# Experts of an expert-choice FFN: tokens fetched by indirect transfers instead of one-hot gather products

## The chip, the cores and the metric

One core of a Trainium2 chip runs the whole program, a four-layer model whose stages follow one another. The metric is the device time of one execution in microseconds.

## The reference, cut to what matters

Layer 2 holds an FFN in which every expert chooses its tokens. With n = 8 batches, t = 256 x 2 = 512 tokens, d = 256, hidden f = 1024, 8 experts:

```python
scores = jnp.einsum('ntd,ed->nte', x, gate_w)
probs = jax.nn.softmax(scores, axis=-1)
g, m = jax.lax.top_k(probs.transpose(0, 2, 1), k)     # k = 2 * 512 / 8 = 128 tokens of each expert and batch
xin = x[batch_idx, m]                                  # [8, 8, 128, 256]
h = jax.nn.gelu(jnp.einsum('nekd,edf->nekf', xin, w1), approximate=False)
h = jnp.einsum('nekf,efd->nekd', h, w2)
out = jnp.zeros((n, t, d), dtype=x.dtype).at[batch_idx, m].add(g[..., None] * h)
```

`x` here is the layer-normed activation `xn`. The layer's output is x + s * silu(out), with s the output of a causal attention over the same `xn`.

## The kernel before, in words

The engines are programmed by hand: each stage is a block with one instruction stream per engine, joined by semaphores, and a barrier of all engines ends it. The stages that matter run in this order:

- **The causal attention** (`stage_causal_attend`, L2566). TensorE makes scores for groups of four heads, VectorE takes row maxima, ScalarE exponentiates. A step handles one group g of one batch b; there are 32. SyncE loads the q, k and v stacks of batch b + 1 as the groups of batch b end (L2638 to L2643). Beside this, VectorE finds the 128 best tokens of each of the 64 pairs of batch and expert (`ExpertChoice.dve`, L2251) with sixteen rounds of three operations, and sets `found` after the last. At the beginning SyncE loads the probabilities, w1 and w2 of expert 0 and the first two batches of xn (`load_ahead`, L2230); after the last attention load it stores the places in DRAM and reads the first two rows of them spread over all partitions (`spread_places`, L2237).
- **The gather products** (`experts_gather`, L2863). Per batch, VectorE splits xn in two fp32r parts (high and low), and makes the one-hot matrix `picks` by comparing the places with the number of each token (L2911). TensorE multiplies: for two halves of d and two halves of the experts, four token tiles times two parts, 128x512 each (L2930): 32 products a batch, 256 in all. ScalarE copies the results to `slots` (L2899), which holds the chosen tokens of all experts and batches, d in the partitions. TensorE also turns the probabilities and places (L2918, L2919).
- **The experts' FFN** (`experts_ffn`, L2936). A unit is one half k of the batches (4 x 128 tokens) of one expert e; 16 units. The operands are pairs of fp32r parts and each product has three passes (`three_passes`, L461; its products stand on L464). In step f of a unit TensorE makes the second product of the unit before (12 products of 128x256, banks 4 to 7) and the first product of this one (6 products of 128x512, banks 0 to 3). ScalarE takes the gelu (L2982). VectorE splits the hidden tile (L448 and L455), splits a slice of w2 (k = 0) or of the next expert's w1 (k = 1), at step 3 splits the next unit's x from `slots` (`split_x`, L3000), and at step 1 copies the output of the last-but-one unit to `slots`, times the probabilities (`outputs`, L3008, L3014). GpSimd has nothing to do. SyncE loads the next expert's weights and, once, the weights of the stage after the next into `choice.late` (`distance.load`, L2165).
- **The scatter** (`experts_scatter`, L3082) adds the outputs to their tokens by one-hot products, with silu on ScalarE and the gating on GpSimd; it reads `place_t`, a slot's tokens in its partition.

## Time and profile before

| what | us |
|---|---|
| median of 3 runs (lowest, highest) | 3902.56 (3898.4, 3906.61) |
| the profiled execution, its own time | 3910.28 |
| its span, first to last instruction | 3908.6 |
| TensorE busy in the span | 3289.4 (84%) |
| VectorE busy | 3101.5 (79%) |
| ScalarE busy | 2306.6 (59%) |
| GpSimd busy | 1647.5 (42%) |

The profile shows one execution. Times on its timeline count from the span's start; a comparison with the runs goes by the execution's own time. PE is TensorE's products, PEld its weight loads, DVE VectorE, ACT ScalarE, POOL GpSimd, SP SyncE; a q behind a name (SPq) is an engine's queue of instructions. A product's duration is longer than its distance to the next one, since products overlap.

### The profile page before, as it was taken

The page shows a single profiled execution, that of the slowest core. Times are in us where ns is not written, and L with a number is a line of the kernel's source. Part 1 is how long each engine was busy: PE and PEld are TensorE (multiplying, and loading weights), DVE is VectorE, ACT ScalarE, POOL GpSimd, SP SyncE. Part 2 cuts the span into 40 slices and gives each one's busy share as a digit, 9 for nine tenths or more (in the row PEclk, how much of TensorE's full clock was granted, in tenths as well). Part 3 has the DMA queues.
Part 4 walks back from the last instruction along what each step waited for, and adds up shares of the span by engine and source line. Part 5 has one row for each costly group of instructions (what it writes and reads, how often), then busy time and mean ns, then how long its engine had stood idle before and what let it go on. Part 6 is the DMA issues. An engine that isn't in the chain of part 4 may idle for free. (4 is left out here: it accounts for less than half of the span.)

```text
span 3908.6 us, 57210 instructions
## 1 busy us (share of the span) xinstructions
PE 3289.4 (84%) x16866; PEld 1768.0 (45%) x16866; DVE 3101.5 (79%) x4970; ACT 2306.6 (59%) x2770; POOL 1647.5 (42%) x785
## 2 busy tenths in 40 slices
PE   6758888888979997869799999799996977777776
PEld 3322333333337876645333343599985751111111
DVE  6869999999987777847589885487767768888887
ACT  4767666666663336724266666222222758999998
POOL 0009998989963110022100000000015338998996
PEclk9879999999999998968699999899998987888888
DMA  4543333333303357838532322221103553344442
GB/s 124 199 192 125 116 131 140 141 141 141 117 30 109 124 153 183 196 106 272 161 79 70 75 73 54 81 64 54 43 28 113 170 174 94 114 124 123 122 117 90
DMA packets 294398, 465.54 MB, mean 119 GB/s; under 512 B 40711, under 2 KB 237960, under 8 KB 273790
## 3 DMA queue, kind: packets, MB, share of 16 engines
q1 hardware_dynamic: 249838, 412.98, 33.0%
q10 hardware_dynamic: 44432, 51.10, 4.9%
q8 instruction: 50, 0.82, 0.1%
q14 instruction: 78, 0.64, 0.1%
HBM read 322.44 MB, written 141.33 MB: 119 GB/s over the span
## 5 line engine op out<-in xcount | busy, mean ns | idle before, releaser
L1225 PE MATMUL mamba_psum<-mamba_hc,scan_ident 128*128 128x512 f32 x1024 | 547.3, 642 | 91.7 <-DVE mamba_hc L1133 74.3
L3643 POOL TENSOR_TENSOR distance_dist<-distance_dist,distance_least_all 128x2048 f32<-128x2048 f32 x124 | 559.1, 4540 | 74.6 <-DMA distance_least_all<-distance_least_rows 74.6
L3126 POOL TENSOR_TENSOR scatter_out<-scatter_out,scatter_s 128x512 f32<-128x512 f32 x16 | 28.0, 1756 | 1032.4 <-ACT scatter_out L3143 1018.0
L1156 DVE TENSOR_TENSOR_SCAN mamba_psum<-mamba_psum,mamba_drive 128x512 f32<-128x512 f32 x352 | 414.8, 1216 | 23.2 <-issue 10.8
L2704 DVE TENSOR_REDUCE causal_row_max<-causal_psum 128x1 f32<-128x512 f32 x512 | 333.2, 683 | 81.5 <-PE causal_psum L2774 72.1
L1225 PEld LDWEIGHTS mamba_psum<-mamba_hc,scan_ident 128*128 128x128 f32 x1024 | 174.8, 195 | 419.3 <-DVE mamba_hc L1133 258.1
L2663 ACT ACTIVATE causal_probs<-causal_psum 128x1024 f32<-128x1024 f32 x256 | 250.9, 1021 | 125.3 <-PE causal_psum L2797 125.2
L3819 PE MATMUL distance_psum<-distance_shared_k_stacks,distance_shared_q_stacks 102*128 102x512 bf16 x512 | 207.8, 502 | 116.6 <-DVE distance_least L3737 56.5
L3737 DVE TENSOR_REDUCE distance_least<-distance_psum 128x2 f32<-128x1024 f32 x256 | 294.1, 1213 | 7.6 <-PE distance_psum L3819 7.3
L3773 DVE TENSOR_SCALAR distance_dist<-distance_psum 128x1024 f32<-128x1024 f32 x192 | 227.0, 1219 | 81.0 <-PE distance_psum L3834 81.0
L1076 POOL TENSOR_TENSOR mamba_drive<-late_channels,scan_b_all 128x1024 f32<-128x1024 f32 x64 | 150.0, 2357 | 287.9 <-POOLq L32 287.9
L1120 ACT ACTIVATE mamba_psum<-mamba_dt,scan_a_neg 128x512 f32<-128x512 f32 x256 | 167.4, 683 | 141.0 <-DVE mamba_hc L1133 140.5
L1120 ACT ACTIVATE mamba_psum<-late_channels,scan_a_neg 128x512 f32<-128x512 f32 x256 | 167.2, 683 | 137.3 <-DVE mamba_hc L1133 129.2
L2982 ACT ACTIVATE ffn_hidden<-experts_psum 128x512 f32<-128x512 f32 x128 | 76.7, 599 | 281.8 <-PE experts_psum L464 281.8
L3714 ACT ACTIVATE distance_dist<-distance_dist 128x2048 f32<-128x2048 f32 x128 | 233.8, 1898 | 0.3
L2773 PE MATMUL causal_psum<-causal_shared_k_stacks,causal_shared_q_stacks 100*128 100x512 bf16 x512 | 194.6, 405 | 29.3 <-DVE causal_row_max L2704 14.7
L1156 DVE TENSOR_TENSOR_SCAN mamba_h<-mamba_psum,mamba_drive 128x512 f32<-128x512 f32 x160 | 193.9, 1212 | 4.6 <-ACT mamba_psum L1120 4.6
L3706 ACT ACTIVATE distance_dist<-distance_dist 128x2048 f32<-128x2048 f32 x96 | 179.3, 1899 | 6.0 <-DVE distance_dist L3773 5.7
L2796 PE MATMUL causal_psum<-causal_shared_q_stacks,causal_shared_k_stacks 103*128 103x512 bf16 x512 | 170.6, 385 | 3.1 <-ACT causal_probs L2663 1.6
L3819 PEld LDWEIGHTS distance_psum<-distance_shared_k_stacks,distance_shared_q_stacks 102*128 102x128 bf16 x512 | 34.3, 105 | 300.3 <-DVE distance_least L3737 198.7
L3855 PE MATMUL distance_psum<-distance_dist,distance_shared_v 128*32 128x512 f32 x1024 | 158.6, 698 | 12.1 <-ACT distance_dist L3714 10.5
L3834 PE MATMUL distance_psum<-distance_shared_q_stacks,distance_shared_k_stacks 102*128 102x512 bf16 x512 | 142.1, 398 | 14.7 <-DVE distance_dist L3773 11.9
(477 smaller groups left out, 8776.0 us busy)
## 6 DMA issues: line engine op xcount, KB each, us to landing
distance_least_all<-distance_least_rows SPq DMA_DIRECT2D x32, 1024.0 KB, 4.6
scan_b_all<-bc SPq DMA_DIRECT2D x16, 1024.0 KB, 4.7
scan_c_all<-bc SPq DMA_DIRECT2D x16, 1024.0 KB, 6.7
mamba_b_all<-bc SPq DMA_DIRECT2D x16, 1024.0 KB, 5.0
mamba_c_all<-bc SPq DMA_DIRECT2D x16, 1024.0 KB, 6.9
choice_w<-L_ffn_w SPq DMA_DIRECT2D x16, 1024.0 KB, 5.6
z<-mamba_in_z SPq DMA_DIRECT2D x8, 1024.0 KB, 3.9
xc<-mamba_in_xc SPq DMA_DIRECT2D x8, 1024.0 KB, 3.9
```

Of the source, the lines that this page charges most:

```text
L1120: act.activation(ps[:, DECAY_BANK + n % RING], dt[slot][:, m], ACT.Exp, scale=a_neg[:, m, s:s + 1]).then_inc(decay_ready, 1)
L1156: dve.tensor_tensor_scan(out, bank, drive[:, n % DRIVES], 0.0, ALU.mult, ALU.add).then_inc(h_ready, 1)
L1225: pe.matmul(ps[:, Y_BANK + m % 2], ident[:, :], hc[:, n % PRODUCTS], start=False, stop=(s == DS - 1)).then_inc(y_summed, 1)
L2663: act.activation(probs[:, g % 2, kt, 2 * pair:2 * pair + 2], ps[:, 2 + n % 2 * 2:4 + n % 2 * 2], ACT.Exp, scale=SCALE).then_inc(p_ready, 1)
L2704: dve.reduce_max(row_max[:, g % 2, u:u + 1], ps[:, u % 2], AX.X).then_inc(a_max, 1)
L2773: pe.matmul(ps[:, u % 2], qs[0:KA, g, h, i * P:(i + 1) * P], ks[0:KA, g, h, :], start=True, stop=False)
L3643: pool.tensor_tensor(dist[:, g % 2, kt], dist[:, g % 2, kt], least_all[:, g % 2], ALU.subtract).then_inc(shifted, 1)
L3706: act.activation(dist[:, g % 2, kt], dist[:, g % 2, kt], ACT.Sqrt).then_inc(sqrt_ready, 1)
L3714: act.activation(dist[:, g % 2, kt], dist[:, g % 2, kt], ACT.Exp, scale=-1.0).then_inc(p_ready, 1)
L3737: dve.tensor_reduce(least[:, g % 2, h * TT + 2 * j:h * TT + 2 * j + 2], ps[:, pair(UNITS + u)], op=ALU.min, axis=AX.X).then_inc(a_min, 1)
L3773: dve.tensor_scalar(dist[:, g % 2, kt, j * 2 * T:(j + 1) * 2 * T], ps[:, pair(u)].rearrange("p h t -> p (h t)"), D2_MIN, None, ALU.max).th ...
L3819: last = pe.matmul(ps[:, pair(UNITS + u)][:, i], qs[0:KD, g, h, (2 * j + i) * P:(2 * j + i + 1) * P], ks[0:KD, g, h, :], start=True, stop= ...
```

## The change

The stage of gather products is gone. The attention's SyncE stores the places before the loads for the last batch, and reads them back transposed (`turn_places`), so that partition j has the j-th token of every pair of batch and expert. GpSimd adds each batch's first row number, converts to integers and fetches for expert 0 the 128 rows of xn of every batch by indirect transfers (`gather`, 128 partitions x 256 f32 each): 4 for each half k, into `raw`, which has one buffer per half. In the FFN GpSimd fetches the rest, 4 transfers after each unit's rows have been turned, 56 in all. A unit's rows are turned on TensorE at steps 3 and 4 of the unit before, four 128x128 blocks a step, into banks 4 to 7, the two that do not collect the present second product. ScalarE rounds each bank into x high, VectorE subtracts it from the bank into x low. Four of the six late weight matrices are loaded where all were, the other two and `wo` after the last turn, since `raw` lies in their place. The removed functions stand in full in the section above; of the diff the new code follows.

```diff
...
+    def load_rest(self, sp):
+        self.load_rows(sp, self.NAMES[self.BELOW_RAW:])
         load_head_columns(sp, self.wo_cols, self.w["wo"], self.loaded)
...
+        self.raw = self.late[:, 2 * TT * D:].rearrange("p (k n d) -> p k n d", k=2, n=NB // 2)
+        self.place_t = c.sb("place_t", [P, NB * NE2])
+        self.first_row = c.sb("first_row", [P, NB * NE2])
+        self.rows = c.sb("rows", [P, NB * NE2], mybir.dt.uint32)
...
-    def spread_places(self, sp):
+
+    def turn_places(self, sp, nc):
         sp.wait_ge(self.found, 1)
-        sp.dma_start(self.place_dram.rearrange("b (e j) -> (b e) j", e=NE2), self.place_f[:, :]).then_inc(self.place_stored, DMA)
+        sp.dma_start(self.place_dram, self.place_f[:, :]).then_inc(self.place_stored, DMA)
         sp.wait_ge(self.place_stored, DMA)
-        for r in range(2):
-            self.load_places(sp, r, r)
+        with nc.allow_non_contiguous_dma(reason="a slot's tokens to its partition, once"):
+            sp.dma_start(self.place_t[:, :], self.place_dram.rearrange("r j -> j r")).then_inc(self.place_loaded, DMA)
 
     def pool(self, pool):
         make_identity(pool, self.ident, self.ident_made)
-        pool.iota(self.token[:, :], [[P, TT]], base=0, channel_multiplier=1,
-                  allow_small_or_imprecise_dtypes=True).then_inc(self.made, 1)
         pool.iota(self.tokens[:, :], [[1, T]], base=0, channel_multiplier=0,
                   allow_small_or_imprecise_dtypes=True).then_inc(self.made, 1)
+        pool.iota(self.first_row[:, :], [[T, NB], [0, NE2]], base=0, channel_multiplier=0,
+                  allow_small_or_imprecise_dtypes=True).then_inc(self.made, 1)
+        pool.wait_ge(self.made, 2)
+        pool.wait_ge(self.place_loaded, DMA)
+        pool.tensor_tensor(self.first_row[:, :], self.place_t[:, :], self.first_row[:, :], ALU.add).then_inc(self.rows_ready, 1)
+        pool.wait_ge(self.rows_ready, 1)
+        pool.tensor_copy(self.rows[:, :], self.first_row[:, :]).then_inc(self.rows_ready, 1)
+        pool.wait_ge(self.rows_ready, 2)
+        for k in range(2):
+            self.gather(pool, 0, k)
+
+    def gather(self, pool, e, k):
+
+        rows = self.xn_in.rearrange("b t d -> (b t) d")
+        for n in range(NB // 2):
+            column = (k * (NB // 2) + n) * NE2 + e
+            pool.indirect_dma_start(
+                out=self.raw[:, k, n, :], out_offset=None, in_=rows,
+                in_offset=bass.IndirectOffsetOnAxis(ap=self.rows[:, column:column + 1], axis=0)).then_inc(self.gathered[k], DMA)
 
...
+                choice.load_ahead(sp)
+                with sp.Fori(0, NB - 2) as b:
+                    load_next(b)
+                choice.turn_places(sp, nc)
+                load_next(NB - 2)
...
-        experts_gather(nc, choice, ps, prob_t, place_t, slots)
...
+        TURN_STEPS = (3, 4)
+
+        def following(e, k):
+            return (e, 1) if k == 0 else (e + 1, 0)
+
+        def turned_bank(k, m):
+            return ps[:, 4 + 2 * (1 - k) + m]
...
-                distance.load(sp, nc)
+                distance.load_first(sp, nc)
                 with sp.Fori(1, NE2 - 1) as e:
                     load_next(e)
+                sp.wait_ge(x_turned, UNITS * DT)
+                distance.load_rest(sp)
+
+            @block.gpsimd
+            def _(pool):
+                for e in range(1, NE2):
+                    for k in range(2):
+                        pool.wait_ge(x_turned, ((e - 1) * 2 + k + 1) * DT)
+                        choice.gather(pool, e, k)
 
             @block.scalar
             def _(act):
+                def round_x(e, k, m):
+
+                    act.wait_ge(x_turned, (e * 2 + k) * DT + m + 1)
+                    act.copy(x_parts.high[:, k, :, m * P:(m + 1) * P],
+                             turned_bank(k, m).rearrange("p (n j) -> p n j", n=HB)).then_inc(x_parts.rounded, 1)
+
                 def body(e, final):
                     for n in range(2 * FT2):
+                        k, f = divmod(n, FT2)
                         tile = e * 2 * FT2 + n
                         act.wait_ge(h_done, tile + 1)
                         wait_past(act, h_parts.ready, tile + 1 - RAW)
                         act.activation(hidden[:, n % RAW], ps[:, n % 4], ACT.Gelu).then_inc(h_ready, 1)
-
+                        if f in TURN_STEPS and not (final and k == 1):
+                            round_x(*following(e, k), TURN_STEPS.index(f))
+
+                act.wait_ge(prob_turned, 1)
+                act.copy(prob_t[:, :], ps[:, 0, 0:NB * NE2]).then_inc(prob_copied, 1)
+                for m in range(DT):
+                    round_x(0, 0, m)
...
+                def rest_of_x(e, k, m):
+
+                    dve.wait_ge(x_parts.rounded, (e * 2 + k) * DT + m + 1)
+                    rows = slice(m * P, (m + 1) * P)
+                    dve.tensor_tensor(x_parts.low[:, k, :, rows], turned_bank(k, m).rearrange("p (n j) -> p n j", n=HB),
+                                      x_parts.high[:, k, :, rows], ALU.subtract).then_inc(x_parts.ready, 1)
...
-                        if f == 3 and not (final and k == 1):
-                            split_x(e + k, 1 - k)
+                        if f - 1 in TURN_STEPS and not (final and k == 1):
+                            rest_of_x(*following(e, k), TURN_STEPS.index(f - 1))
...
+                split_w1(0, 0)
+                for m in range(DT):
+                    rest_of_x(0, 0, m)
+                for f in range(1, FT2):
                     split_w1(0, f)
-                split_x(0, 0)
+                dve.wait_ge(prob_copied, 1)
...
+                def turn_x(e, k, m):
+
+                    if m == 0:
+                        pe.wait_ge(choice.gathered[k], (e + 1) * HB * DMA)
+                        wait_past(pe, o_copied, (e * 2 + k - 2) * HB)
+                    for n in range(HB):
+                        last = pe.transpose(turned_bank(k, m)[:, n * P:(n + 1) * P], choice.raw[:, k, n, m * P:(m + 1) * P],
+                                            choice.ident[:, :])
+                    last.then_inc(x_turned, 1)
...
+                        if f == 0:
+                            pe.wait_ge(x_parts.ready, (e * 2 + k) * DT + DT)
                         if not (isinstance(e, int) and e == 0 and k == 0):
                             second_product(e - 1 + k, 1 - k, f)
+                        if f in TURN_STEPS and not (final and k == 1):
+                            turn_x(*following(e, k), TURN_STEPS.index(f))
                         first_product(e, k, f)
...
+                pe.wait_ge(choice.ident_made, 2)
+                pe.transpose(ps[:, 0, 0:NB * NE2], choice.best[:, :], choice.ident[0:NB * NE2, 0:NB * NE2]).then_inc(prob_turned, 1)
+                for m in range(DT):
+                    turn_x(0, 0, m)
+                pe.wait_ge(prob_copied, 1)
...
```

SyncE at the end of the attention, before: the place store and the two spread reads behind the last load.

```order
L2634 REGISTER_ALU
L357 ISA
L357 DMA causal_shared_v<-v 128x4x128
L2638 REGISTER_ALU
L2638 COMPARE_AND_BRANCH
L2239 DMA experts_place_rows<-choice_place_f 64x128
L2228 DMA choice_late<-experts_place_rows 128x1024 x2
```

And in the change, the same place:

```order
L357 DMA causal_shared_v<-v 128x4x128
L2663 REGISTER_ALU
L2663 COMPARE_AND_BRANCH
L2240 DMA experts_place_rows<-choice_place_f 64x128
L2243 DMA choice_place_t<-experts_place_rows 128x64x1
L339 DMA causal_shared_q_stacks<-q_parts 48x2048
L339 DMA causal_shared_q_stacks<-q_parts 32x2048
L339 DMA causal_shared_q_stacks<-q_parts 16x2048
```

The store and the transposed read now stand ahead of the loads for the last batch (written out once behind the loop).

TensorE at step 3 of the first FFN unit, in the change:

```order
L464 MATMUL experts_psum<-ffn_x_high,ffn_w_high 128x512
L464 MATMUL experts_psum<-ffn_x_low,ffn_w_high 128x512
L464 MATMUL experts_psum<-ffn_x_high,ffn_w_low 128x512
L3029 MATMUL experts_psum<-choice_ident,choice_late 128x128 x4
L464 MATMUL experts_psum<-ffn_x_high,ffn_w_high 128x512
L464 MATMUL experts_psum<-ffn_x_low,ffn_w_high 128x512
```

Before, the products followed one another without the four turns (`choice_late` is the buffer that holds `raw`). GpSimd's stream, empty in the FFN before, now has there:

```order
L2932 UNCONDITIONAL_BRANCH
L2265 DMA choice_late<-xn,choice_rows 128x256 x56
L2915 UNCONDITIONAL_BRANCH
```

## Rows read from the trace of the kernel before

**Rows 1.** Stretches: us, busy PE, PEld, DVE, ACT, POOL, then granted clock, DMA, GB/s

```profile
2447.00:2526.20 79.20, 64.97 (x258) 51.55 (x258) 35.74 (x48) 19.14 (x34) 0.00 (x0) 0.90 0.23 80
2546.80:2896.40 349.60, 349.60 (x2255) 318.76 (x2254) 258.70 (x568) 72.50 (x121) 0.00 (x0) 1.00 0.15 45
...
2690.00:2712.50 22.50, 22.50 (x146) 20.44 (x145) 17.06 (x38) 4.79 (x8) 0.00 (x0) 1.00 0.14 47
```

**Rows 2.** Timeline, borders of the gather stage: start, us, engine, line, output<-inputs

```profile
2447.05 0.34 PE L2918 MATMUL experts_psum<-choice_ident,choice_best 64*128 64x64 f32 x1 [5.59 <-PEq L32]
...
2447.20 0.69 DVE L448 CAST gather_xn_high<-choice_late 128x1024 fp32r<-128x1024 f32 x1 [12.83 <-PEq L2920]
...
2526.25 0.29 DVE L448 CAST ffn_w_high<-choice_w 128x256 fp32r<-128x256 f32 x1 [10.91 <-PEq L32]
...
2526.92 0.29 DVE L448 CAST ffn_w_high<-choice_w 128x256 fp32r<-128x256 f32 x1
```

**Rows 3.** Timeline, the head of the FFN

```profile
2532.40 1.23 DVE L455 TENSOR_TENSOR ffn_x_low<-experts_slots,ffn_x_high 128x1024 fp32r<-128x1024 f32 x1
2533.68 0.79 PE L464 MATMUL experts_psum<-ffn_x_high,ffn_w_high 128*128 128x512 f32 x1 [9.54 <-DVE ffn_x_low L455]
2534.27 0.63 PE L464 MATMUL experts_psum<-ffn_x_low,ffn_w_high 128*128 128x512 f32 x1
...
2537.27 0.43 DVE L448 CAST ffn_h_high<-ffn_hidden 128x512 fp32r<-128x512 f32 x1 [3.65 <-ACT ffn_hidden L2982]
...
2541.18 0.42 DVE L448 CAST ffn_h_high<-ffn_hidden 128x512 fp32r<-128x512 f32 x1
...
2542.90 0.42 DVE L448 CAST ffn_h_high<-ffn_hidden 128x512 fp32r<-128x512 f32 x1
...
2546.80 0.28 PE L464 MATMUL experts_psum<-ffn_w_high,ffn_h_high 128*128 128x256 f32 x1
```

**Rows 4.** Turns on L2522 (causal_in): one group, all 64, and the stretch

```profile
1872.25 1.07 PE L2522 MATMUL causal_in_psum<-means_ident,causal_in_xn 128*128 128x128 f32 x8
...
L2522 PE MATMUL causal_in_psum<-means_ident,causal_in_xn x64: 272/273/477, 1731.9 to 1873.1; 128*128 128x128 f32 x64
...
1870.00:1876.00 6.00, 4.46 (x34) 3.63 (x33) 2.38 (x8) 3.67 (x6) 3.47 (x3) 1.00 1.09 203
```

**Rows 5.** Timeline, steps 1 to 3 of one FFN unit

```profile
2710.64 0.60 ACT L2982 ACTIVATE ffn_hidden<-experts_psum 128x512 f32<-128x512 f32 x1 [2.22 <-PE experts_psum L464]
...
2711.82 0.69 DVE L455 TENSOR_TENSOR ffn_h_low<-ffn_hidden,ffn_h_high 128x512 fp32r<-128x512 f32 x1
...
2713.16 1.66 DVE L3014 TENSOR_SCALAR experts_slots<-experts_psum,experts_prob_t 128x256 f32 x4
...
2713.46 0.60 ACT L2982 ACTIVATE ffn_hidden<-experts_psum 128x512 f32<-128x512 f32 x1 [2.22 <-PE experts_psum L464]
...
2714.61 0.40 PE L464 MATMUL experts_psum<-ffn_x_high,ffn_w_high 128*128 128x512 f32 x1
```

**Rows 6.** GpSimd in the scatter stage (ns min/median/max), and a stretch of the scan

```profile
L3126 POOL TENSOR_TENSOR scatter_out<-scatter_out,scatter_s x16: 1263/1441/4877, 2911.6 to 2992.4; 128x512 f32<-128x512 f32 x16
...
500.00:900.00 400.00, 351.24 (x777) 130.20 (x776) 382.34 (x431) 264.25 (x339) 368.24 (x194) 0.97 0.33 126
```

**Rows 7.** Timeline, SyncE's issues late in the attention, TensorE's first scores of batch 7

```profile
2329.39 1.26 SPq L339 DMA_DIRECT2D causal_shared_q_stacks<-q_parts  x3
...
2346.19 0.38 PE L2773 MATMUL causal_psum<-causal_shared_k_stacks,causal_shared_q_stacks 100*128 100x512 bf16 x1
...
2390.01 0.51 SPq L2239 DMA_DIRECT2D experts_place_rows<-choice_place_f  x1
2392.46 1.10 SPq L2228 DMA_DIRECT2D choice_late<-experts_place_rows  x2
```

**Rows 8.** DMA packets, from 1688 to 1689 and from 1690 to 1692 us

```profile
DMA packets 2101, 0.09 MB, mean 88 GB/s; under 512 B 2038, under 2 KB 2100, under 8 KB 2100
...
DMA packets 872, 0.05 MB, mean 27 GB/s; under 512 B 872, under 2 KB 872, under 8 KB 872
```

108 lines of the change are left out of this document (14 added, 94 removed).

## The prediction

> **What bounds the kernel now.** I read the busy time by stretch first, since a share over the whole span says nothing of one stage. The change touches two stages that follow one another on one core. The first is the stage of gather products: it takes 79.2 us from its first instruction to the first of the experts' FFN [rows 1]. In it TensorE is busy 64.97 us, VectorE 35.74 and ScalarE 19.14, so TensorE is its bound, with starts and stops. The second is the FFN. From its second unit on TensorE is busy 349.6 of 349.6 us at full granted clock, VectorE 258.7, ScalarE 72.5 and GpSimd not at all [rows 1]: whatever the change adds to TensorE there is paid in full, and what it adds to ScalarE and GpSimd is hidden until one of them makes TensorE wait.
>
> Then the timeline at the borders. TensorE and VectorE start the gather stage at 2447.05 and 2447.20, and the FFN's first VectorE instruction stands at 2526.25 [rows 2]. In the FFN's head VectorE works alone: eight splits of w1, 0.67 us each from 2526.25 to 2526.92 [rows 2], then the split of x, which ends at 2533.63, then TensorE starts at 2533.68 [rows 3]. Its first eight products last until the second unit starts at 2546.80 [rows 3]. A unit is half the batches of one expert, 16 in all; in the steady state one step (a second product and a first product) takes 2.82 us, the distance of two gelus [rows 5], so a unit 22.56.
>
> **The change, step by step.**
> 1. The stage goes. From 2447.20 to 2526.25 on VectorE, 79.05 us, with one barrier and the 128 x 2 products, 32 copies and 32 comparisons inside it [rows 1, 2]. What the gather stage waited for before 2447 stays, since the FFN now stands where the gather stood. First term: **-79.05**.
> 2. The FFN's head. TensorE turns the probabilities (0.34 us [rows 2]) and eight blocks of x. A group of eight turns of 128x128 f32 took 1.07 us in an earlier stage, one alone 0.273, so (1.07 - 0.27)/7 = 0.114 per turn at full clock [rows 4]; cold I count double, 0.23. The first four end near 0.34 + 4 x 0.23 + 0.2 = 1.5 us after the start, the second four near 2.4. ScalarE rounds each half (0.6, as a gelu of 128x512 [rows 5]), so the second half at 3.1; VectorE subtracts it (0.69, as for h_low [rows 5]): 3.8. Then TensorE starts, at 3.8 instead of 2533.68 - 2526.25 = 7.4. But VectorE now has seven splits of w1 still to do, 0.67 each: its first h cast comes at 8.45, against 11.0 before (2537.27 [rows 3]). From there it is the slower engine, 1.73 us a tile (2541.18 to 2542.90 [rows 3]), and x of unit 1 is ready after six tiles and two subtractions: 8.45 + 6 x 1.73 + 1.4 = 20.2, against 20.55 before. The 3.6 us won at the start are therefore lost to VectorE again, and the eight turns of unit 0 fit beneath. Second term: **-0.3**.
> 3. Units 1 to 14 each turn eight blocks for their successor: 112 turns on the engine that is always busy, 112 x 0.114 = **+12.8**. The far ends of this price are 0.06, if the weight load of a turn hides as it does between products, and 0.24, the cold rate.
> 4. These turns stand in 28 groups between fp32r products. A refill of the array costs between nothing and the 0.27 of one turn; I take 0.05, since products of both kinds follow one another without a gap in rows 5: **+1.4**.
> 5. A new wait: the turn writes banks of the last-but-one unit's output, so TensorE waits for the four output copies that VectorE makes at step 1. In the trace those run from 2713.16 for 1.66 us, to 2714.82, while TensorE would be at the turn at 2714.61, the start of the first product of step 3 [rows 5]. It is late by 0.2 us, plus the restart; queued behind it is every product of the step. I take 0.3 in each of 14 units: **+4.2**; ends 0 (VectorE a little earlier, since the x split at step 3 becomes cheaper) and 0.5.
> 6. On VectorE the split of x, some 2.0 us (in the head from 2526.25 + 8 x 0.67 to 2533.63), becomes 2 x 0.69; on ScalarE 2 x 0.6 per unit are added to 4.79 busy of 22.5 us [rows 1]. Both are hidden by TensorE. The gelu behind a rounding is later by nothing that anybody waits for: 2.22 us idle stand before each [rows 5].
> 7. The 56 indirect transfers in the FFN run on GpSimd, idle until now. A half of the raw buffer is free 45 us before its rows are wanted, and GpSimd has to serve four transfers per unit of 23.9 us: each may take 6.0 us. The trace has no such row. The nearest are 0.51 us (SyncE's issue of the store of places [rows 7]) and 4.88 (the slowest GpSimd operation of the scatter stage [rows 6]); both are below 6.0. Term: 0.
> 8. SyncE. The table of places is stored and read back transposed before the loads for the last batch, and those queue behind it. The q and k loads for it begin at 2329.39 [rows 7]. Now the store goes first and takes 2.46 us until the next issue (2390.01 to 2392.46 [rows 7]), then the transposed read of 8192 elements of 4 bytes. A stretch with such packets moved 2101 in 1 us [rows 8], so 4 us of transfer. The q and k loads are then issued by about 2335 and land near 2340; TensorE wants them at 2346.19 [rows 7]. Hidden, with 6 us to spare. If small packets run at the 872 in 2 us of the other row, the read takes 19 us and the loads land near 2356: +10. The first eight gathers have until 2447, and 100 us are enough at 12 us each.
> 9. The late weights for the next stage (two of six matrices, eight slices) are loaded after the last turn, more than a unit before the scatter stage, hidden by that unit. The loads of xn and of spread places vanish from a queue that nobody waited for outside the gather stage.
>
> Sum: -79.05 - 0.3 + 12.8 + 1.4 + 4.2 = **-61** us. The profiled execution took 3910.28 (span 3908.6), 7.7 above the median; by its own measure 3849, from the median 3902.56 it is **3841.5**.
>
> The Trainium skill (TensorE: Matmul & The Clock Gate, "Part 4: PE-mode transpose") gives about 275 ns for a transpose in a kernel's context; our 0.273 is the duration of one and 0.114 the distance of two. At 275 ns a turn, 112 would cost 30.8 and the result would be about 3859.5.
>
> **The rivals.**
> A. Turns at the cold rate's price, 0.24 each: +14, 3856. For it: the groups are only four long and each starts with a weight load. Against: the row of eight. Chance 0.10.
> B. The transposed read is slow and the last batch's attention waits: +10, 3852. For: 872 packets in 2 us in one row; against: 2101 in 1 us in another [rows 8]. Chance 0.08.
> C. GpSimd is shut out while VectorE works, and the transfers become the bound; the place is TensorE's wait for the raw rows at step 3. VectorE works 17.06 of 22.5 us [rows 1], so a unit becomes 17.1 + 4g if GpSimd needs g per transfer by itself. It decides from g = 1.7 us, and eats the whole gain where 14 x (17.1 + 4g - 23.9) exceeds 61, from g = 2.8. At the 4.88 of rows 6 a unit takes 36.6, 14 x 12.7 = +178 us against a gain of 61, 4020: slower. For it: a 128x512 GpSimd operation took 1.26 to 4.88 us beside VectorE in the scatter stage [rows 6]. Against: in the scan VectorE is busy 382 and GpSimd 368 of 400 us together [rows 6], which no exclusion allows. Chance 0.05, and 0.03 for a g between that leaves part of the gain (about 3875).
> The Trainium skill (SBUF — State Buffer, "SBUF: two separate sides") says that while VectorE runs a copy in its two-port mode GpSimd cannot write descriptors, and gives some 3.1 us instead of 0.62 for a transfer beside it. By that figure, waiting included, four take 12.4 us of a unit and the sum stays as it is; whether VectorE's casts shut GpSimd out here, no row shows.
> D. TensorE's clock falls at the turns. A cold 128x512 product is 0.63 long, a warm one 0.40 [rows 3, 5]; 14 units at half rate would add some 316 us, 4158. Against: the stretch with eight turns shows a granted clock of 1.00, 2.4 GHz [rows 4]. Chance 0.01. The same section on the transpose says that turns do not count as activity for the clock; here they are 0.9 us of a unit's 23.9.
> E. The change doesn't do what it says in time: the first gathers reach the FFN late because the places or GpSimd's first call are late. The FFN's head would wait; up to 20 us lost, 3862. Chance 0.02.
>
> **The numbers.** 0.71 for the forecast (itself 3828 to 3852: turns at 0.06 and no wait give -73, the waits and refills at their upper ends -50). A, B, E and the mild form of C lie between 3852 and 3875. The range 3827 to 3866 leaves out C, D and part of the tails. A change of 0.2% (8 us) is about what a measurement of this kernel can tell from none. Faster 0.93, same 0.02, slower 0.05.
>
> **What would show it.** The gather lines are gone and the FFN's first instruction stands near 2447. The second unit starts about 20 us later. Gelus stay 2.82 apart but at steps 3 and 4, where 0.46 is added, and at step 3 a wait of some 0.3 for the output copies. A unit takes 23.9 instead of 22.56; from the second unit's start to the last product 349.6 becomes about 368. GpSimd shows four transfers per unit and no instruction waits for them. TensorE's first scores of the last batch are not later than before. The prediction is wrong if TensorE waits for a transfer in the FFN, if turns stand more than 0.2 apart, or if q and k of the last batch are late.

## The result, and the profile after

| | before | after |
|---|---|---|
| median us (lowest to highest, runs) | 3901.98 (3898.4 to 3906.61, 4) | 3840.99 (3839.13 to 3841.78, 4) |
| ratio, 95% interval | | 0.9837 [0.9824, 0.9851] |
| profiled execution, own time | 3910.28 | 3840.4 |
| its span | 3908.6 | 3838.3 |
| gather stage and FFN, first product to the scatter | 2447.05 to 2900.02: 452.97 | 2438.90 to 2827.33: 388.43 |

Faster by 61 us (58 to 69 by the interval), as forecast. The two profiled executions differ by 69.9, and only 64.5 of that lies in the stages that the change rewrote; the table of stretches below shows where the rest comes from.

The stretches of after, columns as in [rows 1]: the whole of it, from the second unit's start to the last gelu, and one pitch between two units' first gelus.

```profile
2438.90:2827.33 388.43, 381.22 (x2434) 344.66 (x2435) 271.18 (x609) 93.49 (x162) 56.06 (x56) 0.99 0.21 62
2459.13:2812.70 353.57, 353.00 (x2275) 320.15 (x2275) 248.74 (x554) 84.52 (x148) 48.12 (x48) 1.00 0.21 62
2636.70:2660.35 23.65, 23.65 (x155) 21.47 (x155) 17.09 (x38) 5.81 (x11) 3.92 (x4) 1.00 0.22 67
```

TensorE is still the bound, at full granted clock. A pitch of 22.5 [rows 1] has become 23.65, and GpSimd is busy 3.92 of it where it did nothing.

The head of the FFN, which answers to [rows 2, 3]; timeline, columns as there:

```profile
2438.90 0.29 DVE L448 CAST ffn_w_high<-choice_w 128x256 fp32r<-128x256 f32 x1 [10.64 <-PEq L32]
...
2439.17 1.97 PE L3029 MATMUL experts_psum<-choice_ident,choice_late 128*128 128x128 f32 x8
...
2442.58 0.77 PE L464 MATMUL experts_psum<-ffn_x_high,ffn_w_high 128*128 128x512 f32 x1 [1.45 <-issue]
...
2447.05 0.42 DVE L448 CAST ffn_h_high<-ffn_hidden 128x512 fp32r<-128x512 f32 x1
...
2459.13 0.39 PE L464 MATMUL experts_psum<-ffn_w_high,ffn_h_high 128*128 128x256 f32 x1 [2.11 <-DVE ffn_x_low L2981]
```

First product 3.7 us after the stage's start, first h cast 8.15, second unit 20.23, where TensorE stands 2.11 us for the subtraction of unit 1's x. The forecast had 3.8, 8.45 and 20.2.

Gelus around the turning steps, which answer to [rows 5]:

```profile
2630.41 0.60 ACT L2953 ACTIVATE ffn_hidden<-experts_psum 128x512 f32<-128x512 f32 x1 [2.22 <-PE experts_psum L464]
2633.23 0.60 ACT L2953 ACTIVATE ffn_hidden<-experts_psum 128x512 f32<-128x512 f32 x1 [2.22 <-PE experts_psum L464]
2636.71 0.60 ACT L2953 ACTIVATE ffn_hidden<-experts_psum 128x512 f32<-128x512 f32 x1 [2.88 <-PE experts_psum L464]
...
2639.98 0.60 ACT L2953 ACTIVATE ffn_hidden<-experts_psum 128x512 f32<-128x512 f32 x1 [2.19 <-PE experts_psum L464]
```

2.82, then 3.48 and 3.27. The second turning step is 0.45 longer, which is four turns of 0.11 (the price that turns_twice below gives) and nothing for changing the kind of product; the first has 0.21 more. The view by tile shows all turns and all indirect transfers (ns min/median/max, first and last start):

```profile
L3029 PE MATMUL experts_psum<-choice_ident,choice_late x128: 271/272/474, 2439.2 to 2780.0; 128*128 128x128 f32 x128
L2265 POOL DMA_INDIRECT choice_late<-xn,choice_rows x64: 942/946/1176, 2333.0 to 2737.1; - x64
```

And the waits in the stage (us in total, times, longest):

```profile
POOL choice_late L2265 <- PE experts_psum L3029: 326.4, 14, 98.5
...
PEld experts_psum L3029 <- DVE experts_slots L2990: 1.8, 6, 0.3
```

The wait for the output copies is there, 0.3 us at the longest and booked in six units only, less than I had put down. An indirect transfer keeps GpSimd for 0.946 us (plus 0.30 between two). GpSimd waits 326.4 us for TensorE; nobody waits for GpSimd.

SyncE before the attention's last batch, and TensorE's first scores of that batch, against [rows 7]:

```profile
2322.92 0.49 SPq L2240 DMA_DIRECT2D experts_place_rows<-choice_place_f  x1
2325.37 0.38 SPq L2243 DMA_DIRECT2D choice_place_t<-experts_place_rows  x1
2325.79 6.28 SPq L339 DMA_DIRECT2D causal_shared_q_stacks<-q_parts  x3
2332.13 1.46 SPq L339 DMA_DIRECT2D causal_shared_k_stacks<-k_parts  x3
...
2340.07 0.38 PE L2795 MATMUL causal_psum<-causal_shared_k_stacks,causal_shared_q_stacks 100*128 100x512 bf16 x1
```

Behind the transposed read the three issues of q took 6.28 us instead of 1.26; the loads were there in time all the same.

### The profile page after: what moved, and what is told of

Read it like the earlier page. It is cut to its first block and busy times, and to the rows that moved or that the text cites. A ratio compares the mean times of both kernels' runs of the same rounds, so it can differ in the third digit from the quotient of the medians.

```text
span 3838.3 us, 56660 instructions
## 1 busy us (share of the span) xinstructions
PE 3246.2 (85%) x16737; PEld 1730.1 (45%) x16737; DVE 3057.9 (80%) x4922; ACT 2302.0 (60%) x2769; POOL 1711.6 (45%) x851
## 5 line engine op out<-in xcount | busy, mean ns | idle before, releaser
L1120 ACT ACTIVATE mamba_psum<-late_channels,scan_a_neg 128x512 f32<-128x512 f32 x256 | 167.2, 683 | 136.7 <-DVE mamba_hc L1133 128.7
L2795 PE MATMUL causal_psum<-causal_shared_k_stacks,causal_shared_q_stacks 100*128 100x512 bf16 x512 | 192.8, 401 | 29.3 <-DVE causal_row_max L2726 14.9
L2265 POOL DMA_INDIRECT choice_late<-xn,choice_rows x64 | 63.8, 998 | 341.6 <-PE experts_psum L3029 326.4
L3851 PE MATMUL distance_psum<-distance_dist,distance_shared_v 128*32 128x512 f32 x1024 | 159.8, 703 | 11.9 <-ACT distance_dist L3710 10.2
```

Source lines behind the costliest of these rows:

```text
L1120: act.activation(ps[:, DECAY_BANK + n % RING], dt[slot][:, m], ACT.Exp, scale=a_neg[:, m, s:s + 1]).then_inc(decay_ready, 1)
L2795: pe.matmul(ps[:, u % 2], qs[0:KA, g, h, i * P:(i + 1) * P], ks[0:KA, g, h, :], start=True, stop=False)
L3851: last = pe.matmul(ps[h * QUAD:(h + 1) * QUAD, 6], v[:, g, kt, h * QUAD:(h + 1) * QUAD], dist[:, g % 2, kt, h * T:(h + 1) * T], start=(kt ...
```

## The experiments

Fourteen profiles, the two above among them, cut at the same events. Columns: from the attention's first row maximum to the cast of the places; from there to the last row maximum, which holds the **last batch**; from there to the experts' **start**; the experts' **stage** to the scatter's first instruction (gather stage included in the kernels before); from there to the end. The experiments ran on three chips, A, B and C; the one of the result above is not known and is called 1. The kernel before had a median of 3901.98 us on chip 1, 3904.62 on A, 3903.19 on B and 3903.66 on C (4, 7, 10 and 15 runs).

| kernel, chip | to cast | last batch | to start | stage | to end | median |
|---|---|---|---|---|---|---|
| before, 1 | 356.6 | 136.7 | 42.65 | 452.97 | 1008.6 | 3901.98 |
| after, 1 | 352.9 | 136.7 | 40.6 | 388.43 | 1011.0 | 3840.99 |
| steps_4_5, A | 352.9 | 143.6 | 40.6 | 400.51 | 1009.3 | 3862.1 |
| turns_twice, A | 353.1 | 142.3 | 42.1 | 404.02 | 1008.9 | 3865.47 |
| places_last, A | 354.9 | 136.8 | 43.4 | 388.07 | 1008.4 | 3846.5 |
| gather_quarters, A | 355.0 | 173.4 | 41.9 | 546.05 | 1010.7 | 4038.71 |
| change_again, B | 353.2 | 142.2 | 43.3 | 389.90 | 1008.8 | 3851.99 |
| gathers_held, B | 352.9 | 136.7 | 43.5 | 388.04 | 1011.9 | 3847.6 |
| head_split_places_last, B | 353.1 | 136.7 | 43.9 | 386.10 | 1010.1 | 3847.68 |
| quarters_spread, B | 354.8 | 172.8 | 40.2 | 424.32 | 1007.6 | 3924.17 |
| gather_halves, C | 353.0 | 136.7 | 40.5 | 389.29 | 1007.5 | 3841.93 |
| quarters_plain, C | 352.8 | 136.7 | 40.2 | 388.64 | 1004.8 | 3839.41 |
| head_split_gathers_held, C | 353.1 | 136.7 | 40.5 | 386.46 | 1010.9 | 3841.42 |
| before_xn_late, C | 352.8 | 136.8 | 40.3 | 455.10 | 1006.0 | 3901.72 |

Read it by columns. "To cast" and "to end" vary by 4 and by 7 us without following an edit, and each kernel has but one profile; I take that for chance of one execution. The stage follows the kernel. The last batch follows the kernel and the chip: the change itself has 136.7 and 142.2. "To start" varies by up to 3 us late in the stretch whatever the kernel, but the 43.4 to 43.9 of places_last, gathers_held and head_split_places_last have a cause of their own, shown below.

### One step later: steps_4_5

```diff
-        TURN_STEPS = (3, 4)
+        TURN_STEPS = (4, 5)
```

> The changed kernel with the turned products of each unit one step later (steps 4 and 5 of eight instead of 3 and 4). Theory (the turns in step 3 wait for the output copies of step 1, about 0.1 to 0.2 us a unit): the time from the last cast of the gelus' first unit to the last unit falls by 0.10 to 0.21 times 14, that is 1.5 to 3 us of the 353.6 measured; in the first unit the turned tokens come one VectorE step later, so that unit starts up to 1.7 us later; sum about -0.5, 3838 to 3843 us, and no wait of TensorE for an output copy in the FFN. Rival (that wait is only where the profile books a wait for the gathers or for the sequencer): the unit pitch stays at 23.6 us and only the first unit's +1.7 is seen. Second rival (the turned tokens, finished in step 6 instead of 5, come late for the next unit): a wait for the subtraction of the low part at each unit's start, 0.5 us or more a unit, 3848 or more.

3862.1 us, ratio 0.9896 [0.9877, 0.9914]. The waits of TensorE in the FFN:

```profile
PE experts_psum L464 <- DVE ffn_x_low L2981: 12.1, 15, 3.8
```

The wait for output copies is gone, as the theory says: both turning steps are now 3.26 us between gelus (2.82 and four turns of 0.11), where the change has mostly 3.37 to 3.50 in the first of them. But the second rival decided. VectorE works a step behind TensorE, its subtraction of the last x half now stands behind step 6's cast, and every unit starts late: from one unit's last gelu to the next one's first it takes mostly 3.49 or 4.00 us, where the change has 2.82 or 2.90. The 12.1 us of waits are not the stage's 12.1: 2.1 of them, before unit 1, stood in the change too. The 14 borders cost 11.9 us, unit 1 begins 1.6 later and its first gelu comes another 1.5 later, and the wait that is gone gives 2.9 back. A turn at steps 3 and 4 that costs some 2.6 us of waiting is the better place. Of the other 9 of the 21 us, 6.9 are the last batch, below.

### The price of a turn: turns_twice

```diff
-                    for n in range(HB):
+                    for n in (*range(HB), *range(HB)):
                         last = pe.transpose(turned_bank(k, m)[:, n * P:(n + 1) * P], choice.raw[:, k, n, m * P:(m + 1) * P],
```

> The changed kernel with each turned product issued twice to the same place: 256 instead of 128. Theory (TensorE is the bound of every unit and a warm turned product costs its pitch of 0.114 us, nothing for the change between kinds of product): 120 more beyond the first unit cost 112 x 0.114 = +12.8 us, the unit pitch goes from 23.6 to 24.5, the time to 3853 to 3855 us. Rival (a group's cost is in its start and end, not in its length): under +5 us. Rival (slots in TensorE's stream are free while it waits for others): 0. Rival (each turned product costs near its 0.27 us of duration): +30.

3865.47 us, ratio 0.9905 [0.9887, 0.9924]. From the second unit's first gelu to the last gelu it takes 362.77 us against 350.41 after: 12.36 for 112 more turns, **0.110 each**, and the unit pitch is 24.53. The first unit's eight cold ones cost 1.7 (first gelu 8.3 us after the start for 6.6). The theory stands; the time came out 11 above its 3854, of which the last batch has 5.6.

### Who moved the last batch: places_last, change_again, gathers_held

```diff
-                with sp.Fori(0, NB - 2) as b:
+                with sp.Fori(0, NB - 1) as b:
                     load_next(b)
                 choice.turn_places(sp, nc)
-                load_next(NB - 2)
```

> The changed kernel with the store and transposed read of the slot indices after the last of the attention's loads instead of ahead of the last batch's. Theory (6.3 us of SyncE's time was hidden both ways): attention's end, the start of the FFN stage and the time do not move by more than the 0.1 per cent that runs differ, 3838 to 3843 us; the first gathers are issued later but still before the attention's end. Rival (SyncE's order is what moved the start of the FFN stage from 2447.05 to 2438.90): the start of that stage goes back toward 2447 and the time to about 3849. Rival (the first gathers now come late): TensorE waits at the first turned product, up to +10.

3846.5 us, ratio 0.9856 [0.9837, 0.9875]. The stage is as after. The start stood at 2448.23, as the rival had it, but near there (2449.6, 2450.1) it stood in the two kernels above too, which keep SyncE's order. In this profile the attention began 4.4 us later and lost 2.0 us to the cast and 2.8 before the start. What does differ on the same chip is the last batch: 136.8, where steps_4_5 and turns_twice have 143.6 and 142.3. So I ran the change itself again, and once with only its first eight transfers held back:

> The changed kernel itself once more, beside the others. Theory (VectorE and ScalarE, which leave the attention's loop for its last batch while GpSimd issues its first eight indirect transfers, are held until those end, and this happened in the last three runs of kernels with this part and not in the first profile of the change by where the code's fetch fell): the attention from its first to its last row maximum takes 489.6 to 497 us and the time is 3841 to 3850 us; with the hold there is a gap of 4 to 6 us before the copy of the projected batch on ScalarE and the first row maximum after it on VectorE. Rival (the hold belongs to the edited kernels): 489.6 us and 3841 us again. The FFN stage from its first turned product to the scatter takes 388.4 us either way.

```diff
+        if held is not None:
+            pool.wait_ge(*held)
         for k in range(2):
             self.gather(pool, 0, k)
...
-                choice.pool(pool)
+                choice.pool(pool, (pv_done, 2 * TT + (NB - 1) * NG * TT + TT))
```

> The changed kernel with the first eight indirect transfers held back until the last batch's first group of the attention is through (GpSimd waits for its products with the values), the store and the transposed read of the indices staying where they are. Theory (GpSimd's run of transfers holds the fetch of VectorE's and ScalarE's code at the loop's exit): no gap of 4 us there, last batch from the indices' cast to the last row maximum 136.7 us instead of 142 to 143.6, the time 3 to 7 us under the changed kernel's of the same call if that one shows the gap. Rival (the transposed read of 8192 elements of 4 bytes on SyncE delays the last batch's loads): the gap stays and 142 us or more. Rival (the gap moves to where the transfers now are): as long in sum, elsewhere in the last batch.

The change itself took 3851.99 us on chip B (ratio 0.9868 [0.9852, 0.9885]), 11 more than on chip 1, and it is not an edited kernel's fault: the gap is there. Timeline of change_again at the exit of the attention's loop:

```profile
2341.41 1.99 PE L2843 MATMUL causal_psum<-causal_shared_wo,causal_ctx 128*128 128x256 f32 x8
...
2343.73 0.94 POOL L2265 DMA_INDIRECT choice_late<-xn,choice_rows  x1 [0.30 <-issue]
2344.98 0.95 POOL L2265 DMA_INDIRECT choice_late<-xn,choice_rows  x1 [0.30 <-issue]
...
2347.64 0.59 ACT L2699 COPY causal_so<-causal_psum 128x512 f32<-128x512 f32 x1 [6.33 <-DMA xn<-chunks_in_xn]
2347.68 1.29 DVE L2726 TENSOR_REDUCE causal_row_max<-causal_psum 128x1 f32<-128x512 f32 x2 [5.50 <-DMA z<-mamba_in_z]
...
2348.43 0.39 PE L2795 MATMUL causal_psum<-causal_shared_k_stacks,causal_shared_q_stacks 100*128 100x512 bf16 x1 [3.92 <-DVE causal_row_max L2726]
```

The same place with the transfers held:

```profile
2343.13 1.99 PE L2845 MATMUL causal_psum<-causal_shared_wo,causal_ctx 128*128 128x256 f32 x8
...
2345.16 0.59 ACT L2701 COPY causal_so<-causal_psum 128x512 f32<-128x512 f32 x1 [2.14 <-PE causal_psum L2845]
2345.44 1.29 DVE L2728 TENSOR_REDUCE causal_row_max<-causal_psum 128x1 f32<-128x512 f32 x2 [1.54 <-PE causal_psum L2798]
```

ScalarE's copy should come 2.03 us after the start of its products (2343.13 to 2345.16) and comes 6.23 after; VectorE stands as long, though its scores are made; both go on within 0.04 us of each other, 1.7 us after GpSimd's last transfer. The releasers named are transfers of stages long past and cannot be what ended it. With the transfers held, or with the places last (they come after the exit too), the last batch is 136.7 or 136.8. SyncE's order is the same in change_again and gathers_held, so the transposed read is acquitted. The eight transfers at that moment are the cause of this gap, on chips A and B (one profile of each kernel, five with the gap and three without); gathers_held took 3847.6 us (3840.0 to 3856.83), ratio 0.9856 [0.9832, 0.9879], which as a time can't be told from the change.

The third rival, that the gap moves to where the transfers now are, came true in part, and the column of the last batch can't show it. In gathers_held and in places_last the eight transfers run from 2405.14 and from 2400.26, about the last row maximum (2403.21 and 2404.80) and after it. On chip B, gathers_held:

```profile
2405.14 1.17 POOL L2267 DMA_INDIRECT choice_late<-xn,choice_rows  x1 [67.62 <-PE causal_psum L2832]
...
2413.49 0.39 PE L2820 MATMUL causal_psum<-causal_shared_q_stacks,causal_shared_k_stacks 103*128 103x512 bf16 x1 [2.29 <-issue]
...
2420.57 0.72 DVE L404 STREAM_TRANSPOSE causal_out_turned<-causal_psum 128x512 f32<-128x512 f32 x1 [14.38 <-PE causal_psum L2832]
```

The same transfers on chip C, head_split_gathers_held (last row maximum at 2402.99):

```profile
2411.51 0.39 PE L2820 MATMUL causal_psum<-causal_shared_q_stacks,causal_shared_k_stacks 103*128 103x512 bf16 x1 [0.53 <-ACT causal_probs L2687]
...
2417.38 0.72 DVE L404 STREAM_TRANSPOSE causal_out_turned<-causal_psum 128x512 f32<-128x512 f32 x1 [11.41 <-PE causal_psum L2832]
```

And on chip A, places_last, 0.15 us after GpSimd's last transfer:

```profile
2410.32 0.58 ACT L2698 COPY causal_so<-causal_psum 128x512 f32<-128x512 f32 x1 [4.75 <-DMA xn<-chunks_in_xn]
```

From the last row maximum to that transpose it takes 14.4 us in eleven of the fourteen profiles, and 17.1, 17.4 and 17.5 in places_last, gathers_held and head_split_places_last, the three on chips A and B whose transfers run there. So moving the eight transfers took away 5.5 to 6.9 us and gave back 2.7 to 3.1. TensorE is among the engines that stand, between two groups of products and far from the loop's exit: what holds the engines goes with the transfers and not with that exit.

### More and smaller transfers: gather_quarters, quarters_spread, gather_halves, quarters_plain

```diff
-            pool.indirect_dma_start(
-                out=self.raw[:, k, n, :], out_offset=None, in_=rows,
...
+            for q in range(self.QUARTERS):
+                part = slice(q * (D // self.QUARTERS), (q + 1) * (D // self.QUARTERS))
+                pool.indirect_dma_start(
+                    out=self.raw[:, k, n, part], out_offset=None, in_=rows,
```

> The changed kernel with each indirect transfer of 128 rows of 1 KB replaced by four of 128 pieces of 256 bytes each, all four by the same indices (so they fetch other numbers than the tokens): 256 indirect transfers instead of 64, as many bytes, four times the packets. Theory (an indirect transfer occupies GpSimd for 0.95 to 1.0 us and 0.3 us of issue, whatever the bytes, and nobody waits for it while four of them take 5 us of a 23.6 us unit): 16 take 20 us a unit, still under the pitch, and the time stays within 3 us of 3841, since a unit's tokens are due 19 us or so after they are asked for; where it does not fit, TensorE waits for the gathers by what exceeds that, at most 4 us a unit. Rival (GpSimd and VectorE hinder each other, in proportion to GpSimd's busy time): VectorE's casts, 0.445 us in the mean against 0.425 before, go above 0.48 and where VectorE is not the bound nothing is seen, but the transfers themselves take over 1.3 us and TensorE waits: 3860 or more. Rival (the cost goes by bytes): transfers of 0.3 us and no change at all.

4038.71 us, ratio 1.0348 [1.033, 1.0367]: slower than the kernel before. Both theories had the size wrong. A transfer of 256-byte pieces takes GpSimd the same 0.947 us (median) as one of 1 KB, so 16 fit into a unit; yet the stage grew by 158 us and the last batch by 37. The timeline in a run of 16 transfers:

```profile
2540.80 1.18 POOL L2268 DMA_INDIRECT choice_late<-xn,choice_rows  x1 [16.60 <-PE experts_psum L3032]
...
2547.58 0.60 ACT L2956 ACTIVATE ffn_hidden<-experts_psum 128x512 f32<-128x512 f32 x1 [2.22 <-PE experts_psum L464]
...
2559.50 0.60 ACT L2956 ACTIVATE ffn_hidden<-experts_psum 128x512 f32<-128x512 f32 x1 [11.32 <-DMA causal_shared_k_stacks<-k_parts]
...
2560.13 0.48 DVE L448 CAST ffn_h_high<-ffn_hidden 128x512 fp32r<-128x512 f32 x1 [9.86 <-issue]
...
2560.15 0.95 POOL L2268 DMA_INDIRECT choice_late<-xn,choice_rows  x1 [0.30 <-issue]
```

ScalarE has no gelu for 11 us with, as at the loop's exit, a releaser that cannot be one; it is booked 30 such waits, 234.4 us, in the stage. TensorE is booked no wait for a transfer, but 98.6 us in 97 waits that nothing in the profile ends, one of 10.99:

```profile
2510.14 0.58 PE L464 MATMUL experts_psum<-ffn_w_high,ffn_h_high 128*128 128x256 f32 x1 [10.99 <-issue]
```

Whether it stands behind the others there or is held itself, the profile does not tell. Its products are slower too: the granted clock of the stage is 0.85 instead of 0.99, and TensorE is busy for 439 us instead of 381, 58 of the 158.

> The kernel with 16 indirect transfers of 256-byte pieces a unit again, now two at a time with a wait for the next of the unit's first products between the pairs, so that GpSimd rests about 0.4 us in each 2.95 us. Theory (while GpSimd issues one indirect transfer after the other, the fetch of other engines' code and SyncE's loads are held to the end of the run, up to 13 us; a break lets them through): gaps of ScalarE fall from 13.6 to under 4 us and the time from 4039 to 3845 to 3900. Rival (it is the share of GpSimd's time, 20 of 23.6 us, that the others are held out): 4000 or more, as before. Rival (the first eight, now 32 without a break at the attention's end, cost what was lost): about 40 us stay of it in either case, which is seen apart: the attention's last batch 170 instead of 137 us.

```diff
+                if pause is not None and q % 2 == 0:
+                    pause(n * 2 + q // 2)
```

3924.17 us, ratio 1.005 [1.0033, 1.0066]. The stage is 424.3 instead of 546.1 (on another chip, though, and where GpSimd was late its pauses closed up); such gaps of ScalarE fell from 234.4 to 71.3 us but one of 17.8 was left, so the breaks seem to help and my "under 4 us" missed. The first 32 transfers, not spread, cost the last batch 36 us in both.

> The changed kernel with each indirect transfer made of two of 512-byte pieces (by indices that fetch other numbers than the tokens): 8 a unit, 10 us of GpSimd without a break where the change has 5 and the kernel with quarters 20. Theory (code of the other engines is not fetched while GpSimd's run of indirect transfers lasts, and what an engine has in store covers about the 5 us of the change but not 20): between the two, gaps of some us where a fetch falls into a run, the FFN stage between 388 us (all covered) and 470 us (half of what 20 us runs cost); the last batch of the attention, with a first run of 16, some 15 us longer than the change's. Rival (the loss goes by the share of GpSimd's time over some bound, 20 of 23.6 us being over it and 10 under): 388 to 391 us for the FFN stage.

> The kernel with 16 transfers of 256-byte pieces a unit again, issued by GpSimd as plain transfers of fixed tokens instead of indirect ones (so the experts compute on other tokens). Theory (what holds the others' code and SyncE's loads is the indirect kind, whose descriptors GpSimd itself writes): no gaps over 2 us, FFN stage 388 to 391 us, time 3838 to 3853 us. Rival (it is the number of small packets or of transfers on GpSimd's queue): gaps as with the indirect quarters, FFN stage over 450 us. It also prices the indirect issue itself: 0.95 us of GpSimd's time against what a plain issue takes.

```diff
-                pool.indirect_dma_start(
...
+                pool.dma_start(self.raw[:, k, n, part],
+                               self.xn_in.rearrange("b t d -> (b t) d")[tile * P:(tile + 1) * P, part]).then_inc(self.gathered[k], DMA)
```

On chip C neither shows a gap. Halves: 3841.93 us, ratio 0.9837 [0.981, 0.9863], last batch 136.7 where I expected 15 more, stage 389.3. Its loop exit, with transfers of GpSimd on both sides:

```profile
2343.08 0.58 ACT L2702 COPY causal_so<-causal_psum 128x512 f32<-128x512 f32 x1 [2.14 <-PE causal_psum L2846]
...
2343.35 1.29 DVE L2729 TENSOR_REDUCE causal_row_max<-causal_psum 128x1 f32<-128x512 f32 x2 [1.55 <-PE causal_psum L2799]
...
2343.43 0.94 POOL L2268 DMA_INDIRECT choice_late<-xn,choice_rows  x1 [0.30 <-issue]
```

So a run of transfers at that exit is needed for the gap, and not enough: it came on chips A and B in all five kernels that have the transfers there, and neither in the one such kernel on chip C nor in the profile on chip 1. Plain quarters: 3839.41 us, ratio 0.983 [0.9803, 0.9857], stage 388.6. One plain issue takes GpSimd 0.534 us against 0.956 in the halves:

```profile
L2268 POOL DMA_DIRECT2D choice_late<-xn x224: 534/534/759, 2443.3 to 2743.2; - x112
```

As even the halves ran free on that chip, this run does not tell whether plain transfers would hold the others where indirect ones do. Nor do the halves tell that 8 transfers a unit are harmless on chips A and B, where they were not run.

### The loads left out at the attention's start: before_xn_late

```diff
         self.load_w2(sp, 0)
-        for r in range(2):
-            self.load_xn(sp, r, r)
...
     def spread_places(self, sp):
+        for r in range(2):
+            self.load_xn(sp, r, r)
```

> The kernel before with its two loads of xn (512 KB each) issued after the last of the attention's loads instead of at the attention's start. Theory (the change left these loads out, and they slowed the attention's first loads: from its first row maximum to the first turn of a finished group it takes 60.2 us before and 56.5 to 56.7 us, once 58.5, in kernels with the change): 56.5 us, and the time 2 to 4 us under the kernel before's. Rival (the 3.7 us were chance in one profile): 60 us or any value between, the time the same.

To the first turn of a finished group: 1913.32 to 1969.70, 56.4 us as the theory has it, against 60.2. The time, 3901.72 us, ratio 0.9995 [0.9984, 1.0005], is 1.9 us under the kernel before's, and its interval reaches from 6 us less to 2 more: it excludes neither the theory's 2 to 4 us nor none. Values between (354.8 to 355.0 to the cast) stand in three kernels without those loads, so this stretch varies by 2 us of itself. Whether the 3.7 us of the one profile of before belong to the gain stays open.

### A better kernel: head_split_places_last, head_split_gathers_held

```diff
+        def turn_steps(e, k):
+            return (1, 2) if isinstance(e, int) and e == 0 and k == 0 else (3, 4)
...
+                def high_w1(f):
+                    part = (slice(None), slice(None), slice(f * P, (f + 1) * P))
+                    act.copy(w1_parts.high[part], w1[part]).then_inc(w1_parts.rounded, 1)
...
+                high_w1(0)
+                high_w1(1)
                 for m in range(DT):
                     round_x(0, 0, m)
+                for f in range(2, FT2):
+                    high_w1(f)
```

> The changed kernel with three edits: the places stored and read after the last of the attention's loads; in the first unit of the FFN the turned products at steps 1 and 2 instead of 3 and 4; and the first expert's eight high parts of w1 rounded on ScalarE instead of VectorE. Theory (unit 1 starts 20.2 us after the stage because VectorE's first unit is full and the turned tokens of unit 1 stand behind its steps 4 and 5): unit 1 starts 16 to 18 us after the stage's start, the FFN stage takes 384 to 386.5 us instead of 388.4, and with no gap at the attention's last batch the time is 3 to 8 us under the changed kernel's of the same call. Rival (TensorE in its slow first 5 us bounds the first unit: products at 0.43 us): 388 us. Rival (ScalarE's casts delay its first activation behind its table load): 388 to 389 us.

> The changed kernel with the first eight indirect transfers held until the last batch's first group is through and with the two edits to the FFN's first unit (turned products at steps 1 and 2, high parts of w1 on ScalarE). Theory (both gains stand by themselves): no gap at the loop's exit, last batch 136.7 us; FFN stage 386.1 us; together 7 to 8 us under the changed kernel of the same chip state, 3840 to 3848 us, ratio 0.984 to 0.986 where the change's was 0.9868 in the second call and 0.9837 in the first. Rival (the held transfers hold others later): a gap elsewhere and no gain over placing the indices last.

The first took 3847.68 us, ratio 0.985 [0.9833, 0.9867]; the second 3841.42, ratio 0.9834 [0.9817, 0.9852]. Second unit in the latter, 18.37 us after the start (17.97 in the former, 20.1 for the change on chip B), and no wait before it:

```profile
2461.87 0.28 PE L464 MATMUL experts_psum<-ffn_w_high,ffn_h_high 128*128 128x256 f32 x1
```

The stage is 386.1 and 386.5 instead of 388.4 and 389.9, and the last batch 136.7. Both beat the kernel before. Against the change they win 2 us in the stage where the change shows no gap. On chip B it is some 6: 3.8 in the stage and 5.5 in the last batch, less the 3.1 that the moved transfers cost behind it. There the first one's four runs (3840.35 to 3848.14) all lie under the change's four (3851.08 to 3854.66), though the intervals of the two ratios overlap. The second ran on chip C, where the change itself was not run, so that holding its transfers back is worth anything there is not shown.

## Why the prediction was right, and where it was off

1. **The stage goes, -79.05, and the head, -0.3**: to the second unit's start 99.75 us before (2447.05 to 2546.80), 20.23 now: -79.5 for -79.35. The head was right in its parts too: it is VectorE that fills it, shown by giving its casts to ScalarE and moving two subtractions forward, which won 2 us.
2. **112 turns, +12.8**: 12.36 by doubling them. Rival A, the cold price of 0.24, is out. The Trainium skill (TensorE: Matmul & The Clock Gate, "Part 4: PE-mode transpose") gives 275 ns: as a duration the trace agrees (272), as a cost the doubling says 0.110.
3. **28 refills, +1.4**: nothing; the second turning step, and both of them in steps_4_5, are longer by just their four turns.
4. **The wait for output copies, +4.2**: the step that was mis-sized. From the second unit's start to the last gelu 338.60 us became 353.53, so terms 3 to 5 cost 14.9 for 18.4; less 12.4 for the turns, 2.6 are left, 0.18 a unit for my 0.3. I had taken the distance between VectorE's last copy and the turn from one unit, 0.2, and added a restart for which 0.18 leaves no room. steps_4_5 shows that it is this wait: without it the first turning step is as short as the second.
5. **GpSimd, 0**: 1.25 us a transfer with its pause, well under the limit of 6.0. Rival C is out as put: transfers beside VectorE's casts take 0.942 to 1.176, not 4.88. The Trainium skill (SBUF — State Buffer, "SBUF: two separate sides") gives 3.1 us beside a copy; no run shows that here. Rival D is out too: the granted clock is 1.00 over a unit with its eight turns, 23.65 us.
6. **SyncE, 0 with 6 us to spare**: right in the end and too light in one part. The places' read held the next issues 6.28 us, not 4, and the loads were in time. But the price I had put on rival B, an attention that waits in its last batch, exists: +5.5 to 6.9 us on chips A and B, by another mechanism in the same place. I had asked only whether the first gathers were early enough for the FFN (they were, rival E is out), not whom they disturb where they run. That is the question this step lacked.
7. **The sum**: -61 foreseen, -64.5 in the stages; terms 3 to 5, put 3.5 too high, are the difference. The medians on chip 1 differ by -61.0, and that this is the forecast to the decimal is luck: 3.5 us of the stages' gain do not show in them, and no run says where they are. On chip B the medians differ by -51.2; of the 9.8 us that are missing against chip 1, 5.5 are the gap and 1.5 the stage (389.90 for 388.43), the rest is open. The two profiles' 69.9 hold another 5.75 in "to cast" and "to start" (356.6 and 42.65, against 352.9 and 40.6); the profiled execution of before lay 8.3 above its median.
8. Two slips in the sum's details change nothing: seven splits of 0.67 behind 3.8 end at 8.49 and not 8.45, and the upper ends of refill and wait (28 x 0.27, 14 x 0.5) make -52 and not -50.

## What stays open

What holds the engines is not shown. At the loop's exit VectorE and ScalarE stand with their inputs ready while GpSimd issues transfers, and go on together; a fetch of their next instructions that waits behind the transfers would look like this, and I had expected that. The Trainium skill (Runtime: NRT & Kernel Launch, "Instruction fetch mechanics") says that a taken branch out of the window in store forces a fetch by DMA before the engine can go on, and no run here shows the wait to be that. Three things in the traces speak against it, or at least against that alone. The hold also comes away from a loop's exit, where the transfers were moved to. In the gap of gather_quarters (2548 to 2559.5) the 16 DMA engines are busy for 13.5% of the time, all of it with GpSimd's own packets, so a fetch would not have had to queue for them. And although the DMA view of these executions lists instruction packets, on two queues, it has none in that gap nor in the one of change_again (2341.4 to 2347.6); whose fetches those queues carry it does not say.

Why chip 1 and chip C have no gap with as many transfers is open too, and so is whether plain transfers would be free of it on chips A and B.

## What to carry to other kernels

Replacing 256 one-hot products by fetches by index paid because the turns that it adds cost their distance (0.11 us), not their duration (0.27), and because the fetches lie on an idle engine. Keep the runs of such fetches short: runs of four, with rests between, cost the FFN at most 1.6 us in all, while a run of eight cost the attention 5.5 to 6.9 us in one place and 2.7 to 3.1 in another on two chips, and nothing on the others. Use whole rows: the cost is per transfer, whatever its bytes. Compare profiles by stretches between the same events and on more than one chip before a few us are put down to an edit, and when work is moved, look for its cost where it went and not only where it was.

## What the runs showed of the hardware, unexpected

- An indirect transfer of 128 rows keeps GpSimd 0.946 us in the median with 1 KB pieces (after), 0.956 with 512 bytes (gather_halves) and 0.947 with 256 (gather_quarters), plus 0.30 between two; a plain one of 256-byte pieces 0.534 (quarters_plain).
- Beside runs of 16 indirect transfers ScalarE stood for up to 13.6 us at a time (chip A) with nothing that the profile shows to wait for. Beside runs of eight, engines stood for 2.7 to 6.9 us on chips A and B and not at all on C. Runs of 4, 5 us long, cost the FFN nothing in most kernels and 1.6 us in all in change_again.
- Behind a transposed read of 8192 elements of 4 bytes, SyncE's next three issues took 6.28 us instead of 1.26.
